# Attention: sums taken with the exponentials, values of two rows weighed behind the scores, the gate as a tangent

## The reference, cut to the attention

```python
q = split_heads(q_x @ Wq) / math.sqrt(C_HID)
k = split_heads(kv_x @ Wk)
v = split_heads(kv_x @ Wv)
a = jnp.einsum('bnhqc,bnhkc->bnhqk', q, k)
a = a + mask_bias + tri_bias
a = jax.nn.softmax(a, axis=-1)
o = jnp.einsum('bnhqk,bnhkc->bnhqc', a, v)
...
g = jax.nn.sigmoid(q_x @ Wg).reshape(lead + (H, C_HID))
o = o * g
...
return o @ Wo
```

## Time and profile before

| | |
|---|---|
| median of 3 runs | 4782.44 us (4778.9 to 4783.41) |
| the profiled execution | 4780.51 us |
| its span | 4778.3 us |
| mean granted TensorE clock | 0.957 |
| busy, share of the span | PE 92%, PEld 69%, DVE 71%, ACT 60%, POOL 55% |

### The profile page before, as it was taken

One profiled execution on the slowest core, in us unless ns is written; L12 is line 12 of the kernel. 1 busy time (PEld: TensorE's weight loads), 2 busy tenths in 40 slices (PEclk: granted clock), 3 DMA queues, 4 the chain that ended last, 5 costly groups with the idle time before them and its releaser, 6 DMA issues. The chain is left out here.

```text
span 4778.3 us, 107900 instructions
## 1 busy us (share of the span) xinstructions
PE 4404.8 (92%) x36006; PEld 3300.3 (69%) x36006; DVE 3389.0 (71%) x9795; ACT 2866.4 (60%) x6430; POOL 2616.7 (55%) x2043
## 2 busy tenths in 40 slices
PE   6999999999999999777899989999749997999995
PEld 5777777777777777544677766777423446999995
DVE  7888888888888888651566666666427994666766
ACT  0888888888888888412333333333326883666665
POOL 0999999999999999402233322333105661122222
PEclk8999999999999999887899999999879998999997
DMA  7222222222222222497322222222566887999995
GB/s 312 66 74 75 74 75 74 76 73 74 74 75 74 76 73 77 173 383 258 108 72 73 71 86 69 71 73 71 203 229 212 291 292 254 268 287 292 289 290 131
DMA packets 754787, 713.02 MB, mean 149 GB/s; under 512 B 60694, under 2 KB 635413, under 8 KB 745688
## 3 DMA queue, kind: packets, MB, share of 16 engines
q1 hardware_dynamic: 735723, 672.74, 45.7%
q10 hardware_dynamic: 14717, 20.01, 1.2%
q0 software_dynamic: 3808, 13.47, 0.7%
HBM read 506.70 MB, written 199.29 MB: 148 GB/s over the span
## 5 line engine op out<-in xcount | busy, mean ns | idle before, releaser
L309 POOL TENSOR_TENSOR at_bias<-at_tri,at_mask 128x1024 f32<-128x1024 f32 x512 | 1216.9, 2377 | 26.3 <-DMA at_mask<-in_L_conv_mask_bias_dram 10.6
L427 ACT ACTIVATE at_probs<-at_neg_s,at_neg_max 128x256 f32<-128x256 f32 x2048 | 870.9, 505 | 0.7 <-DVE at_neg_max L478 0.7
L478 DVE CUSTOM_DVE_ANT_0 at_neg_s<-at_p_s,at_bias 128x256 f32<-128x256 f32 x2048 | 759.8, 418 | 7.6 <-PE at_p_s L350 2.9
L301 POOL TENSOR_TENSOR at_paired_t<-at_probs_t 128x512 f32<-128x512 f32 x512 | 658.2, 1286 | 9.1 <-ACT at_probs_t L419 4.9
L969 ACT ACTIVATE ml_h<-ml_p_turns,l_b 128x512 f32<-128x512 f32 x384 | 263.8, 687 | 608.9 <-PE ml_p_turns L928 608.9
L361 PE MATMUL at_p_t<-all_ident,at_probs 128*128 128x128 f32 x4096 | 628.2, 276 | 0.6 <-DVE at_probs_t L486 0.4
L361 PEld LDWEIGHTS at_p_t<-all_ident,at_probs 128*128 128x128 f32 x4096 | 476.0, 141 | 131.7 <-issue 104.1
L1070 POOL TENSOR_TENSOR ml_x2t<-ml_z,ml_xb 128x512 f32<-128x512 f32 x128 | 163.9, 1280 | 677.6 <-DVE ml_z L1036 677.6
L937 PEld LDWEIGHTS ml_p<-l_w1s,ml_h 128*128 128x128 f32 x4096 | 471.9, 192 | 52.7 <-issue 52.7
L1997 POOL TENSOR_TENSOR dw_room<-dw_room,all_b_plain 128x512 f32<-128x512 f32 x128 | 178.1, 1392 | 592.1 <-DMA dw_room<-x3t 592.0
L928 PE MATMUL ml_p_turns<-ml_h,l_w 128*128 128x512 f32 x1024 | 487.2, 599 | 2.3 <-DVE ml_h L1002 2.3
(11 more groups left out here) (230 smaller groups left out, 9168.8 us busy)
## 6 DMA issues: line engine op xcount, KB each, us to landing
dw_xw<-planes SPq DMA_DIRECT2D x128, 528.0 KB, 4.7
sp_xs<-x SPq DMA_DIRECT2D x128, 512.0 KB, 9.1
dw_wts<-patch_w SPq DMA_DIRECT2D x128, 512.0 KB, 6.2
planes<-pw_plane SPq DMA_DIRECT2D x128, 264.0 KB, 3.0
in_xs<-in_x_dram SPq DMA_DIRECT2D x32, 1024.0 KB, 7.7
at_xs<-in_x_dram SPq DMA_DIRECT2D x256, 128.0 KB, 2.5
at_kvs<-in_L_conv_kv_x_dram SPq DMA_DIRECT2D x256, 128.0 KB, 2.7
at_mask<-in_L_conv_mask_bias_dram SPq DMA_DIRECT2D x256, 128.0 KB, 3.3
```

Source lines behind the costliest of these rows:

```text
L301: pool.tensor_tensor(paired_t[:, n % 2, part], probs_t[:, n % 3, part, 0], probs_t[:, n % 3, part, 1], ALU.add).then_inc(paired, 1)
L309: pool.tensor_tensor(bias[:, n % 2, part], tri[:, part], mask[:, n % 4].unsqueeze(1).broadcast_to((128, 4, COLS)), ALU.add).then_inc(maske ...
L427: e = act.activation(probs[:, h, qh, :], neg_s[:, n % 2, h, qh, :], ACT.Exp, bias=neg_max[:, n % 2, i:i + 1], scale=-1.0)
L478: t = dve.tensor_tensor_reduce(neg_s[:, n % 2, h, qh, :], p_s[h][:, qh, :], bias[:, n % 2, i, :], -1.0, 3.0e38, ALU.add, ALU.min, neg_max[ ...
```

## The change

The sum of a query's exponentials is no longer made on TensorE from paired, transposed exponentials. Each exponential activation delivers it as its accumulator (`accum_out`) in `sums`. For two rows at once VectorE takes the reciprocals (`invert`, 16 values per partition), GpSimd repeats each 32 times (`spread_sums`), and TensorE transposes the result (`turn_sums`) into the bank `p_t[0]`, between two uses of it by `turn_probs`. VectorE multiplies it there by 1 + tanh(g/2) (`denominator`), and `gate` multiplies by 0.5 and the weighed values, since sigmoid(g) = 0.5 (1 + tanh(g/2)). Ln and Exp of `invert`, GpSimd's `pair` and the matmuls with `ones` are gone, and the table set loaded at the start of the stage is one with exp and tanh.

`weigh`, `gate`, `project_out`, `residual` and the store handle two rows in one visit. `pair_at(n, lag)` gives the pair in every second iteration: `turn_sums`, `invert` and `spread_sums` with lag 2 (even n), `weigh`, `denominator` and `gate` with lag 3 (odd n), `project_out` and `residual` with lag 4 (even n), the store with lag 5. On TensorE `weigh` moves from behind `project_vg` to behind `score`; `turn_sums` is last in its iteration. `turn_probs(n, 0)` waits for `den_made`. On ScalarE `exps(n+1, 0)` comes ahead of `read_qk(n+2)` in the iterations that weigh. On VectorE the third head's copy `read_probs(n, 2)` stands behind three heads of `add_bias`, and in even iterations ahead of `residual` and the fourth head. The rings of x and kv have 10 rows instead of 8, those of values and gate 6 instead of 4, of transposed exponentials 4 instead of 3. The diff, cut:

```diff
+        probs_t = m.sb("probs_t", [128, 4, HEADS, HALVES, COLS])
+        sums = m.sb("sums", [128, 4, HALVES, HEADS])
+        parts = m.sb("parts", [128, 2, 2, HALVES, HEADS])
+        spread = m.sb("spread", [128, 2, 2, HALVES, HEADS, HEAD_DIM])
+        og = m.sb("og", [128, 2, 2, COLS])
         x1s = m.sb("x1s", [128, 4, HALVES, CH])
...
+        def pair_at(n, lag):
+
+            return (n - lag) // 2 if n % 2 == lag % 2 and lag <= n < rows + lag else None
...
-            def pair(n, half):
...
+            def spread_sums(q):
+                pool.wait_ge(inverted, q + 1)
+                if q >= 2:
+                    pool.wait_ge(sums_turned, q - 1)
+                pool.tensor_copy(spread[:, q % 2].rearrange("p r q h d -> p (r q h) d"),
+                                 parts[:, q % 2].rearrange("p r q h -> p (r q h)").unsqueeze(2).broadcast_to(
+                                     (128, 2 * HALVES * HEADS, HEAD_DIM))).then_inc(sums_spread, 1)
...
-                for half in range(2):
-                    if exists(n - 1):
-                        pair(n - 1, half)
-                    if exists(n + 2):
-                        add_mask(n + 2, half)
+                if exists(n + 2):
+                    add_mask(n + 2, 0)
+                q = pair_at(n, 2)
+                if q is not None:
+                    spread_sums(q)
+                if exists(n + 2):
+                    add_mask(n + 2, 1)
...
+                if h == 0 and n >= 3:
+                    pe.wait_ge(den_made, (n - 1) // 2)
...
+            def turn_sums(q):
+                pe.wait_ge(sums_spread, q + 1)
+                pe.wait_ge(even_read, min(4 * q + 6, 2 * rows))
+                for r in range(2):
+                    for half in range(HALVES):
+                        mm = pe.transpose(p_t[0][:, r, half * 128:(half + 1) * 128],
+                                          spread[:, q % 2, r, half].rearrange("p h d -> p (h d)"), ident[:, :])
+                mm.then_inc(sums_turned, 1)
+
+            def weigh(q):
+                pe.wait_ge(even_read, 4 * q + 4)
+                pe.wait_ge(odd_read, 4 * q + 4)
+                pe.wait_ge(vg_read, 2 * q + 2)
+                if q >= 1:
+                    pe.wait_ge(x1_made, q)
+                for r in range(2):
+                    n = 2 * q + r
+                    for kh in range(HALVES):
+                        for h in range(HEADS):
+                            ch = slice(HEAD_DIM * h, HEAD_DIM * (h + 1))
+                            mm = pe.matmul(p_out[ch, r, :], vs[:, n % 6, kh, ch], probs_t[:, n % 4, h, kh, :],
+                                           start=kh == 0, stop=kh == HALVES - 1)
                 mm.then_inc(weighed, 1)
...
             pe.wait_ge(const_loaded, 16 * 6)
-            pe.wait_ge(cleared, 1)
-            for n in range(-2, rows + 2):
+            for n in range(-2, rows + 3):
                 if exists(n + 1):
                     project_vg(n + 1)
-                if exists(n - 2):
-                    weigh(n - 2)
                 if exists(n):
                     turn_probs(n, 0)
                 if exists(n + 2):
...
                     turn_probs(n, 1)
                 if exists(n + 1):
                     score(n + 1)
+                q = pair_at(n, 3)
+                if q is not None:
+                    weigh(q)
                 if exists(n + 2):
                     project_qk(n + 2)
                 if exists(n):
                     turn_probs(n, 2)
-                if exists(n - 2):
-                    project_out(n - 2)
+                q = pair_at(n, 4)
+                if q is not None:
+                    project_out(q)
                 if exists(n):
                     turn_probs(n, 3)
+                q = pair_at(n, 2)
+                if q is not None:
+                    turn_sums(q)
...
-            act.preload_act_table_set(EXP_LN_SET)
+            act.preload_act_table_set(EXP_TANH_SET)
...
             def exps(n, h):
                 act.wait_ge(biased, n * HEADS + h + 1)
                 if n >= 1:
                     act.wait_ge(p_turned, (n - 1) * HEADS + h + 1)
+                if n >= 4:
+                    act.wait_ge(inverted, (n - 4) // 2 + 1)
                 for qh in range(HALVES):
                     i = h * HALVES + qh
                     e = act.activation(probs[:, h, qh, :], neg_s[:, n % 2, h, qh, :], ACT.Exp,
-                                       bias=neg_max[:, n % 2, i:i + 1], scale=-1.0)
+                                       bias=neg_max[:, n % 2, i:i + 1], scale=-1.0,
+                                       accum_out=sums[:, n % 4, qh, h:h + 1])
                 e.then_inc(exped, 1)
-
-            def invert(n):
...
+                if n >= 6:
+                    act.wait_ge(gated, (n - 6) // 2 + 1)
+                act.activation(vs[:, n % 6], p_in[:, 0, :], ACT.Copy)
+                act.activation(gate_t[:, n % 6], p_in[:, 1, :], ACT.Tanh, scale=0.5).then_inc(vg_read, 1)
             for n in range(-2, rows + 2):
                 if exists(n + 1):
...
                     exps(n, 1)
                     exps(n, 2)
                     exps(n, 3)
-                if exists(n - 2):
-                    invert(n - 2)
                 if exists(n):
                     read_probs(n, 1)
+                weighing = pair_at(n, 3) is not None
+                if weighing and exists(n + 1):
+                    exps(n + 1, 0)
                 if exists(n + 2):
                     read_qk(n + 2)
-                if exists(n + 1):
+                if not weighing and exists(n + 1):
                     exps(n + 1, 0)
                 if exists(n):
                     read_probs(n, 3)
...
             def read_probs(n, h):
                 dve.wait_ge(p_turned, n * HEADS + h + 1)
...
+            def invert(q):
+                dve.wait_ge(exped, (2 * q + 2) * HEADS)
+                if q >= 2:
+                    dve.wait_ge(sums_spread, q - 1)
+                at = 2 * q % 4
+                dve.reciprocal(parts[:, q % 2], sums[:, at:at + 2]).then_inc(inverted, 1)
+
+            def denominator(q):
+                dve.wait_ge(sums_turned, q + 1)
+                dve.wait_ge(vg_read, 2 * q + 2)
+                if q >= 2:
+                    dve.wait_ge(gated, q - 1)
+                dve.scalar_tensor_tensor(out=den[:, q % 2], in0=gate_t[:, 2 * q % 6:2 * q % 6 + 2], scalar=1.0, in1=p_t[0][:, :, :],
                                          op0=ALU.add, op1=ALU.mult).then_inc(den_made, 1)
...
+            def gate(q):
+                dve.wait_ge(weighed, q + 1)
+                dve.wait_ge(den_made, q + 1)
+                if q >= 2:
+                    dve.wait_ge(out_made, q - 1)
+                dve.scalar_tensor_tensor(out=og[:, q % 2], in0=p_out[:, :, :], scalar=0.5, in1=den[:, q % 2],
+                                         op0=ALU.mult, op1=ALU.mult).then_inc(gated, 1)
+
+            def residual(q):
+                dve.wait_ge(out_made, q + 1)
...
+                at = 2 * q % held
+                dve.tensor_tensor(x1s[:, q % 2 * 2:q % 2 * 2 + 2].rearrange("p r h c -> p (r h c)"),
+                                  p_out[:, :, :].rearrange("p r k -> p (r k)"),
+                                  xs[:, at:at + 2].rearrange("p r h c -> p (r h c)"), ALU.add).then_inc(x1_made, 1)
...
-            for n in range(-2, rows + 2):
-                if exists(n - 2):
-                    denominator(n - 2)
+            for n in range(-2, rows + 3):
+                inverting, weighing, leaving = pair_at(n, 2), pair_at(n, 3), pair_at(n, 4)
+                if weighing is not None:
+                    denominator(weighing)
                 if exists(n):
                     read_probs(n, 0)
+                if inverting is not None:
+                    invert(inverting)
                 if exists(n + 2):
                     read_turn(n + 2)
-                if exists(n - 2):
-                    gate(n - 2)
                 if exists(n + 1):
                     add_bias(n + 1, 0)
                     add_bias(n + 1, 1)
-                if exists(n - 2):
-                    residual(n - 2)
-                if exists(n + 1):
                     add_bias(n + 1, 2)
+                if weighing is not None:
+                    if exists(n + 1):
+                        add_bias(n + 1, 3)
+                    gate(weighing)
                 if exists(n):
                     read_probs(n, 2)
-                if exists(n + 1):
+                if leaving is not None:
+                    residual(leaving)
+                if weighing is None and exists(n + 1):
                     add_bias(n + 1, 3)
```

More of the change, by code:

```diff
@@ L211, in attention @@
     maskv = mask_bias[0].rearrange("r a b k -> r (a b) k")
+    held, pairs = 10, rows // 2
     with ExitStack() as ctx:
@@ L278, in _ @@
                 load_mask(n)
-            for n in range(-2, rows + 2):
+            for n in range(-2, rows + 5):
```

(41 more changed lines are left out.)

75 lines of the change are left out of this document (28 added, 47 removed).

## The result

| | before | after |
|---|---|---|
| median of 4 runs | 4780.67 us | 4990.15 us |
| lowest to highest | 4777.31 to 4783.41 | 4987.4 to 4995.34 |
| profiled execution, its span | 4780.51, 4778.3 | 4992.1, 4990.0 |

The changed kernel is slower: 1.0436 times, 95% interval 1.0424 to 1.0449. The forecast was 5000 us, in a range from 4905 to 5070.

What follows compares the result with a forecast made beforehand. TensorE's order was taken as the bound, and it would wait for ScalarE's exponentials: 8.01 + 8.18 = 16.19 us per two rows, 0.865 more per row over 254 rows, +220 on 4780.5, 5000 us; range 4905 to 5070.

Steps and rivals of the forecast that it cites:

- The bound: Attention stage: TensorE's order binds, GpSimd just behind; after the change TensorE stands about 1 us in each row.
- The even iteration: Loop from project_vg to project_vg without weighing: 2.86 + 0.58 + 4.07 + 0.50 = 8.01 us.
- The odd iteration: Loop from project_vg to project_vg with the weighing of two rows behind score: 8.18 us together.
- The accumulator: ScalarE's sum read after each exponential: 0.09 us, eight per row, 0.18 us on the path TensorE waits for.
- The cover of the denominator: Odd iteration: turn_probs(n, 0) waiting for VectorE's denominator costs nothing, with 0.2 to 0.5 us to spare.
- one of the prediction's signs of being wrong: List of waits after the change: prediction wrong if the longest wait is for VectorE's denominator.
- (a): Rival: TensorE's order stays dense, 6.86 us per row, 0.37 less, 4687 us; chance 0.04.
- (b): Rival: only turn binds because exponentials come out sooner; 0.44 us less per row, 4889 us; chance 0.05.
- (c): Rival: ScalarE's accumulator read at 0.20 us gives 5056 us, at zero 4954; within bounds, part of the forecast's 0.86.
- (d): Rival: tanh and exp not in one table set, two loads per row, 2.57 us per row, 5650 us; chance 0.01.
- (e): Rival: VectorE's denominator later than its cover, each 0.3 more is 38 us, 5040; within bounds, part of 0.86.

Runs made afterwards that it cites:

- the covered order: Changed kernel with second-head exponentials ahead of read_vg, second turn_probs ahead of turn, third-head copy and denominator earlier on VectorE: 4719.7 to 4734.22 us, 0.988 times before.

## Why the prediction was right

**The bound.** TensorE's order, dense before, was the bound, and the wait that replaced it is the one that was named: in every row for `at_probs`. Moving the exponentials alone took it away and 113 us with it.

**The even iteration** was taken as 8.01 us and took 7.98: 2.86 to the second `turn_probs` (2.86 taken), 0.59 to `score` (0.58), 4.07 to `turn_sums` (4.07, VectorE's way, and the run with the earlier copy shows TensorE's at 3.81 as worked out), 0.46 to `project_vg`. Only the last term was off: 0.50 was taken, with 0.06 for starting from a wait, and here that costs 0.02.

**The odd iteration** was taken as 8.18 and took 8.18: 2.77 (2.75), 0.59 (0.58), 1.07 (1.08), 1.87 (1.89), 1.88 (1.88). The change from `score`'s tiling to that of the weighing, which no row of before showed, took the same as the one to full tiles: 1.07 here, 1.08 from `score` to `project_qk` in the even iteration. The Trainium skill (TensorEngine Tiling (Array Packing), Key Properties) has a change of mode drain TensorE. The trace agrees in so far as this change costs 0.19 us (1.07 for 0.88 of work); no row shows that a drain is what it goes on.

**The accumulator** was taken as 0.09, from VectorE's read of 0.08. Its record lasts 0.194, nearly the upper bound of 0.20, and whoever summed records would have been at 5056 us. But the exponentials start every 0.49 us (1002.74, 1003.23, 1003.72) where they started every 0.40 without it, and the run without accumulators found 0.18 for two: 0.09. The row nearest in kind was the right choice, and it was luck in part: nothing in the trace of before said that the record would overlap the next instruction by half.

**The cover of the denominator** was taken as 0.2 to 0.5 us. The first `turn_probs` of the odd iteration waits for it until `project_vg` + 1.42, which without the wait for `at_probs` puts the second at + 2.35 (the run with the early exponentials); it starts at + 2.77. The cover is 0.42. VectorE's 512-wide operations took 0.68 (683 ns is the mean of the 128 at L524), 0.05 less than the row they were taken from.

**The rest.** GpSimd is busy for 62% (60 to 70 taken), its copy took 0.61; neither shows on TensorE. ScalarE's work was to stay at about 6.2 us per row and came to 6.4 (393.78 us over 61.9 rows), without effect. The total was 8 us too high in the profiled execution (5000 against 4992.1): 4 from the 0.03 us too much in each pair, 4 from what follows the loop, which came out 3.8 us shorter and had been left at nothing.

**Signs that were not as told.** Accumulator reads of about 0.09 us were expected, and the records have 0.194. The waits of TensorE for ScalarE were to come to some 1 us per row, and the list has 0.45 (31.3 and 25.0 over 124 rows). Two things are in this: the records hide a part of each stop, and in odd iterations the first half of the standing is for the denominator. By the starts, TensorE stands 0.56 and 0.44 us for ScalarE in the even iteration (`turn` comes 1.00 behind the first `turn_probs`, the second `turn_probs` 0.88 behind `turn`, where a group takes 0.44), and in the odd one 0.54 for the denominator (1.42 for 0.88 of work) and 0.44 for the exponentials: 0.72 per row for ScalarE, 0.27 for VectorE. In the odd iteration the listed wait for the denominator, 0.37, is thus longer than the one for the exponentials, 0.25, which comes close to one of the prediction's signs of being wrong. It was not one, because the exponentials end last: moving them away shortens the odd iteration to 7.70 us, and the run with the earlier copy lets the first `turn_probs` wait 0.42 us longer for the denominator and still takes 8.17.

**The rivals.** (a) TensorE dense: not in this order; the covered order comes within 39 us of its 4687 (4725.67; a pair of 14.08 where it has 13.7), so it was an account of the work and not of the schedule. (b) `turn` alone binding: false as the kernel stands, true in even iterations as soon as the exponentials are early. (c) the accumulator: decided at 0.09. (d) tanh and exp in two sets: false; the stage has one table load of 1.28 us, so they share a set. The Trainium skill says so too (ScalarE: Activation LUTs, Table sets: the hidden batching unit), and the trace agrees. (e) VectorE late by more than its cover: not reached, but with the copy earlier the two were level.

## What to carry to other kernels

When an engine is full and the others are not, what stands between its groups of work is cover for the others' steps: before a block is moved, count what is left between a producer and the next use of its result, and look in the first rows of the stage, where that block is not yet there, for what the uncovered step takes. Work that is removed pays only if the orders of the other engines are moved along with it: here the same change was 4.4% slower in one order and 1.2% faster in another. And look at where an added cost stands in its engine's queue rather than at its sum.

## What the hardware showed that was not expected

An accumulator read behind a 128x256 activation has a record of 194 ns but puts off the next start by only 0.09 us (0.49 instead of 0.40 from start to start).

A start after a wait cost TensorE more in one place than in another: 0.02 us at `turn_sums` (0.46 to the next group instead of 0.44), but 0.06 at the second `turn_probs` (0.59 to `score`, and 0.53 in the run with the early exponentials, from 1001.59 to 1002.12, where it does not wait).

Room on an engine that is not the bound is larger than it looks: ScalarE went from 428 to 479 us of 500, and VectorE's waits for it from 46.5 to 122.4 us in 1000, and the loop became 1.1 us longer.
